# Another order of small matmuls inside their bursts, and Gelu ahead of a square on ScalarE, in a fused two-layer network

## The reference, cut to what matters

```python
x = attn_layer(shift_tokens(x), Wqkv[i], q_scale[i], k_scale[i], Wo[i]) + x
x = ffn_layer(shift_tokens(x), ln_g[i], ln_b[i], W1[i], b1[i], W2[i], b2[i]) + x
...
# attn_layer: 16 heads of 64, q and k normalised and rotated, windows of 32 tokens
sim = jnp.einsum('bhwie,bhwje->bhwij', bq, bk2) * QK_SCALE   # 32 queries x 64 keys
attn = jax.nn.softmax(sim, -1)
out = jnp.einsum('bhwij,bhwje->bhwie', attn, bv2)
...
# ffn_layer: 128 -> 2 x 341 -> 128
hg = xn @ W1 + b1
a, gate = jnp.split(hg, 2, -1)
return a * jax.nn.gelu(gate, approximate=False) @ W2 + b2
```

## Time and profile before

| | us |
|---|---|
| median of three runs | 1846.3 |
| lowest and highest | 1843.38 and 1856.85 |
| the profiled execution | 1840.72 |
| its span, first to last instruction | 1838.8 |

### The profile page before, as it was taken

How to read it: one execution, slowest core, us unless ns; L and a number is a source line. 1 busy time by engine, 2 the same in 40 slices (tenths; PEclk the granted TensorE clock), 3 DMA queues, 4 the chain that set the end, 5 groups by cost and what they waited for, 6 DMA issues and landing times. The chain is left out here.

```text
span 1838.8 us, 70687 instructions
## 1 busy us (share of the span) xinstructions
PE 1759.5 (96%) x30348; PEld 1138.0 (62%) x30348; DVE 1454.6 (79%) x1677; ACT 1161.2 (63%) x2031; POOL 1190.7 (65%) x1285
## 2 busy tenths in 40 slices
PE   7988999999999999999999999999999999998788
PEld 6855665665566666566566556656656656655466
DVE  6588788788788878888878878888787888886485
ACT  4356667667666765766766766666576676575554
POOL 1059677687677787767777767767776776775000
PEclk8899999999999999999999999999999999999999
DMA  4013222323222332223323223223223222222031
GB/s 149 1 50 78 56 72 68 91 66 78 73 67 62 93 80 74 68 56 94 80 66 80 64 65 99 67 67 80 69 59 91 71 75 69 66 68 76 2 70 48
DMA packets 87669, 128.94 MB, mean 70 GB/s; under 512 B 26776, under 2 KB 32800, under 8 KB 87360
## 3 DMA queue, kind: packets, MB, share of 16 engines
q1 hardware_dynamic: 87360, 124.43, 26.1%
HBM read 25.70 MB, written 1.11 MB: 15 GB/s over the span
## 5 line engine op out<-in xcount | busy, mean ns | idle before, releaser
L487 POOL TENSOR_TENSOR lent<-t,lent 128x1024 f32<-128x1024 f32 x192 | 455.2, 2371 | 355.8 <-DVE lent L955 355.2
L478 POOL TENSOR_TENSOR lent<-lent,rn 128x512 f32<-128x512 f32 x384 | 400.6, 1074 | 13.8
L618 PEld LDWEIGHTS sc_ps<-shared,v_win 64*64 64x64 f32 x12288 | 197.6, 135 | 147.8 <-issue 146.9
L570 PE MATMUL ring<-ident,lent 128*128 128x128 f32 x1536 | 241.3, 280 | 17.6 <-ACT gel L826 12.5
L570 PEld LDWEIGHTS ring<-ident,lent 128*128 128x128 f32 x1536 | 176.3, 140 | 131.4 <-issue 91.0
L495 POOL TENSOR_TENSOR shared<-shared,rden 128x512 f32<-128x512 f32 x192 | 196.5, 1045 | 90.1 <-DVE rden L939 90.1
L791 ACT ACTIVATE sq<-qk_ps 128x1024 f32<-128x1024 f32 x192 | 196.3, 1023 | 92.4 <-PE qk_ps L555 92.0
L784 ACT COPY shared<-ring 128x512 f32<-128x512 f32 x192 | 111.2, 580 | 197.4 <-PE ring L602 196.8
L955 DVE TENSOR_TENSOR lent<-qk_ps,rot 128x1024 f32<-128x1024 f32 x192 | 232.5, 1211 | 0.0
L965 DVE TENSOR_REDUCE sums<-sq 128x16 f32<-128x1024 f32 x192 | 231.8, 1208 | 0.0
L951 DVE TENSOR_TENSOR t<-qk_ps,rot 128x1024 f32<-128x1024 f32 x192 | 229.2, 1194 | 0.3 <-ACT sq L791 0.2
(11 more groups left out here) (209 smaller groups left out, 2665.2 us busy)
## 6 DMA issues: line engine op xcount, KB each, us to landing
v_win<-v_tok SPq DMA_DIRECT2D x1488, 64.0 KB
wqkv<-in_w_qkv SPq DMA_DIRECT2D x18, 512.0 KB, 3.7
spread<-gate_rows SPq DMA_DIRECT2D x32, 128.0 KB, 3.6
wo<-in_w_o SPq DMA_DIRECT2D x6, 512.0 KB, 4.0
w<-in_w SPq DMA_DIRECT2D x6, 341.0 KB, 3.2
w<-in_w SPq DMA_DIRECT2D x6, 192.0 KB, 2.9
r_xtok<-in_x SPq DMA_DIRECT2D x4, 256.0 KB, 4.2
out_x<-xo SPq DMA_DIRECT2D x4, 256.0 KB, 2.3
```

Source lines behind the costliest of these rows:

```text
L478: nc.gpsimd.tensor_tensor(by_head(quarter(qkn, f)), by_head(quarter(qkn, f)), rn[:, 8 * f:8 * (f + 1)].unsqueeze(2).to_broadcast([P, 8, DH ...
L487: nc.gpsimd.tensor_tensor(half(qkn, k), half(t1, k), half(t2, k), ALU.add).then_inc((q_added, k_added)[k], 1)
L570: ins = nc.tensor.transpose(to[:, n * P:(n + 1) * P], qkn[:, c * P:(c + 1) * P], ident[:, :])
L618: ins = nc.tensor.matmul(sc_ps[64 * par:64 * (par + 1), part, P * pair + WIN * q:P * pair + WIN * (q + 1)], v_win[64 * part:64 * (part + 1 ...
```

## The change

Three hunks. In `scores`, the loop over the four windows now goes inside a loop over `par_first`, and `par` alternates with the window. In `attend`, the four matmuls of a window come in another order. On ScalarE, Gelu 0 comes before the squares of q in stages with `up`. No instruction is added or removed, and no operand changes.

```diff
--- before.py
+++ after.py
@@ -583,8 +583,9 @@
                     if g > 1:
                         pe.wait_ge(oT_copied, 2 * (g - 1))
                 for pair in range(4 * f, 4 * (f + 1)):
-                    for q in range(TW):
-                        for par in range(2):
+                    for par_first in range(2):
+                        for q in range(TW):
+                            par = (par_first + q) % 2
                             ins = nc.tensor.matmul(
                                 sc_ps[WIN * q:WIN * (q + 1), par, 64 * pair:64 * (pair + 1)],
                                 qT[64 * par:64 * (par + 1), pair, WIN * q:WIN * (q + 1)],
@@ -612,14 +613,13 @@
                     pe.wait_ge(sc_sub, 2 * min(g + 2, TILE_COUNT))
                 for pair in range(2 * f, 2 * (f + 1)):
                     for q in range(TW):
-                        for par in range(2):
+                        for par, part in ((0, 0), (1, 1), (0, 1), (1, 0)):
                             n = 2 * pair + par
-                            for part in range(2):
-                                ins = nc.tensor.matmul(
-                                    sc_ps[64 * par:64 * (par + 1), part, P * pair + WIN * q:P * pair + WIN * (q + 1)],
-                                    v_win[64 * part:64 * (part + 1), TW * t + q, DH * n:DH * (n + 1)],
-                                    prT[64 * part:64 * (part + 1), n, WIN * q:WIN * (q + 1)],
-                                    start=True, stop=True)
+                            ins = nc.tensor.matmul(
+                                sc_ps[64 * par:64 * (par + 1), part, P * pair + WIN * q:P * pair + WIN * (q + 1)],
+                                v_win[64 * part:64 * (part + 1), TW * t + q, DH * n:DH * (n + 1)],
+                                prT[64 * part:64 * (part + 1), n, WIN * q:WIN * (q + 1)],
+                                start=True, stop=True)
                 if f == 1:
                     ins.then_inc(av_full, 1)
 
@@ -849,10 +849,9 @@
                     exponentials(g - 2, 1)
                 if up is not None:
                     nc.scalar.preload_act_table_set(GELU_SET)
+                    gelu(up, 0)
                 if tile_there(g):
                     squares(g, 0)
-                if up is not None:
-                    gelu(up, 0)
                 if tile_there(g - 1):
                     copy_qkT(g - 1, 1)
                 if tile_there(g):
```

## The result

The changed kernel takes 1833.0 us (median of 10 runs, 1826.3 to 1840.0) against 1850.6 us (10 runs, 1843.4 to 1857.7): a ratio of 0.9904, with a 95% interval of 0.9882 to 0.9926. The ratio stands for 17.8 us less (13.7 to 21.8), where 15.8 was forecast; the gain is clear of noise, and just inside the 1% that was called no change. The kernel before has a higher median over ten runs than over the three that the forecast stood on, 1850.6 against 1846.3.

What follows compares the result with a forecast made beforehand. TensorE, with work for 96% of the span, was taken to bound the kernel. Bursts 0, Gelu 0.64 plus 0.08 us, 0.72 x 22 = 15.8 us, off the three-run median 1846.3: 1830.5 us; range 1806 to 1850.

Steps and rivals of the forecast that it cites:

- The bursts cost nothing either way: AV (L618) and score (L588) bursts: the new orders of the first two hunks were each costed at 0.
- all four quadrants load weights at once: AV bursts: four records in 58 ns, each quadrant loading for its full time, so order can't fill them more; 0.
- The rival of neighbouring columns: Both bursts: neighbours sharing columns limit the pace; small case 17 us gained (1814), full 37 us (1793); chance 0.28.
- The rival of same-row neighbours: AV and score bursts: each same-row neighbour costs a step, 167 and 75 us in full, 2072 us; chance 0.12.
- Eight tiles full: First part of a score burst: eight records take about 56 ns, so all eight tiles are busy; scores costed at 0.
- Gelu ahead takes the wait of the transposes away: Feed-forward stages: Gelu 0 starts 0.92 us earlier, AV alone bounds the transposes, TensorE gains 0.64 us, 22 times.
- Gate 1 stays 1.66 us behind the transposes, so that surplus is lost: Next gate matmul needs the transposes' bank, copied by ScalarE, so the projection's gain beyond 0.64 us is lost.
- the upper end: Gelu stages: 20.2 us gained if all 0.92 us of Gelu's advance came through.
- The 0.08 us for the linear matmul's weight load: Before AV's second half: the weight load no longer waits for the copy of v; 0.08 us a stage.
- The squares of q are not missed: ScalarE: q's squares are ready 0.6 to 0.7 us later, but VectorE turns q only 4.5 us behind; lower end 0.
- The Gelu gain is given back: Rival, same stage: the transposes' copy comes late or GpSimd's scaling keeps its time; 1840 to 1848 us, chance 0.10.

Runs made afterwards that it cites:

- experiment 2: The kernel before with the first two hunks alone (new burst orders, Gelu unmoved): 1847.1 us against 1844.8, ratio 1.0012.
- experiment 3: The changed kernel with burst neighbours on the same rows wherever possible, in AV and scores: 1826.1 us, ratio 0.9908 to the kernel before.
- experiment 5: The changed kernel with every AV matmul cut in two along its moving side, 16 moving columns each, same 64 weight columns: 2077 us in one run.
- experiment 6: The changed kernel with every AV matmul cut in two along its weight side, 32 weight columns each, eight tiles in turn: 1998 us in one run.
- experiment 4: The changed kernel with AV's loops turned round, each quadrant getting the four windows of a pair in a row: 2084 us in one run.
- experiment 8: The changed kernel with every score matmul cut in two along its moving side, 32 moving columns each: 2144 us.
- experiment 7: The changed kernel with VectorE's product of Gelu 0 moved behind the sum of k's squares: 1830.7 us in one run.

## Why the prediction was right, and where it was not

- **The bursts cost nothing either way: right, and shown.** Experiments 2 and 3 leave the pace unchanged to the record. The reason given was that all four quadrants load weights at once, each for its full time. Experiments 5 and 6 show that AV's pace is the weight load, and experiment 4 fits a quadrant that takes its records in turn. The rival of neighbouring columns falls: experiment 2's interval leaves it 0.04% of the kernel, 1 us. The rival of same-row neighbours, the one that ended slower, has 0.3% left, 5 us of the 242 in its price.
- **"Eight tiles full" in the first part of a score burst: right, though the working clashes.** The prediction read 112 ns as the time of 128 weight columns for AV and, a paragraph on, as that of 128 moving columns for the scores. Both hold, since the earlier trace rows have as many or more weight columns than moving ones and experiment 8 shows the moving columns at work where they are the more. It also counts 192 AV bursts in one place and 190 in another; the trace has 192, and no result hangs on it.
- **Gelu ahead takes the wait of the transposes away: right.** 0.64 us forecast, 0.64 us in the trace, and AV alone bounds the transposes after the change.
- **"Gate 1 stays 1.66 us behind the transposes, so that surplus is lost": wrong.** Gate 1 comes 887.96 - 886.58 = 1.38 us behind them. I took the distance for a chain over ScalarE's copy of the transposes. But in the earlier trace rows that copy had begun at 887.88 and took 0.59, so it was there at 888.47, while gate 1 started at 888.88: it was not waiting for the copy but stood behind v's projection, which had itself waited for VectorE's product, and that for Gelu. Gate 1's first weight load did wait for the copy, but began 0.36 us ahead of its matmul (first row, before). After the change the copy ends at 887.86, the load follows at 887.91 (second row) and gate 1 starts at 887.96: now the copy bounds it, if narrowly, as v's projection would have let it start some 0.03 us sooner by the 0.86 us from gate 0 to linear 0.

```profile
888.52 0.19 PEld L649 LDWEIGHTS ring<-xn,w 128*128 128x128 f32 x1 [0.31 <-ACT qT L773]
```

```profile
887.91 0.30 PEld L649 LDWEIGHTS ring<-xn,w 128*128 128x128 f32 x2 [0.61 <-ACT qT L773]
```

  The whole 0.92 us of Gelu's advance came through, the upper end that the prediction had priced at 20.2 us. Experiment 7 shows the chain from the other side: a later product leaves the transposes alone and moves all that follows by 0.36 us.
- **The 0.08 us for the linear matmul's weight load** was counted beside the 0.64. Part of it is there (888.87 to 889.86 is 0.99 us, 1.03 before), but the total is set by the chain, so it was no term of its own.
- **The squares of q are not missed: right.** They end 0.6 us later (887.08 instead of 886.49), and the copy behind them still waits 0.20 us for its transposes. The stage's gain of 0.92 us shows that nothing on TensorE's way is held up by them.
- **The Gelu gain is given back: no.** The medians of the three other kinds of stages are unchanged to 10 ns.

By these terms the sum should have read 1850.6 - 20.2 = 1830.4 on the median of ten runs; the measurement gives 1833.0, and the kernel with the third hunk alone a ratio that stands for 21.4 us (16.8 to 26.0). That the forecast of 1830.5 is the same number is luck: its base, the median of three runs, was 4.3 us too low, and its gain 4.4 us too small. No version among these beats both kernels beyond its interval: the third hunk alone is as good as the whole change.

## What to carry to other kernels

Small matmuls on tiles of the array run side by side when the tiles take turns; count the tiles that are busy at once from the pace of the starts and the time that one record holds its tile before reordering neighbours, for if all are busy, no order helps, and four matmuls in a row on one tile hurt (2.25 us a burst instead of 0.92). Where one engine's result frees several things on TensorE's way, follow each of them to the last that starts late: here the wait that the profile named was 0.64 us of gain, the advance of the releaser 0.92, and all of the 0.92 came through. To ask what bounds an instruction, compare its start with the end of each of its releasers, not with the start of its neighbour.

## What the runs showed of the hardware that I had not expected

- **The look-ahead seems to pass over whole matmuls, but not far.** With the quadrants in turn, records start in groups of four, 7 ns apart, then 39 ns pass: 58 ns for four. Had each matmul's two records to start one behind the other on the same quadrant before the next matmul's, every second record would come 58 ns late. This takes the two records to stand side by side in the program, which the trace doesn't show. With four matmuls in a row on one quadrant, the burst takes 2.25 us instead of 0.92, not the 3.7 of no overlap at all.
- **Behind the first 32 records of a burst on eight tiles stands a hole,** 0.08 us with the scores as they are and 0.11 with 32 moving columns, and then the records come at 8 to 10 ns each whatever they cost the array (experiments 6 and 8). I read this as the rate at which TensorE gets its instructions; it hangs on their number and not on their columns, but what makes the hole stays open.
- **TensorE can run out of instructions.** Besides the hole there are waits for nothing that the profile names, at much the same places in every execution. A long one in a burst of 128 records of the changed kernel (TensorE, 14 records still to come):

```profile
941.73 1.45 PE L589 MATMUL sc_ps<-kT,qT 64*32 64x64 f32 x114
945.51 0.42 PE L589 MATMUL sc_ps<-kT,qT 64*32 64x64 f32 x14 [2.33 <-issue]
```

A transfer of the instruction queue (16 KB) begins at 942.76 and takes 1.46 us in this execution. It ends at 944.22, and 1.29 us later TensorE goes on. The other traces say the same. In all eleven there are 306 pauses of over 0.6 us between two records of one burst, and 304 of them end 1.15 to 1.65 us after such a transfer ended (the last one to end 0.5 us or more ahead); of moments taken at random, 7 to 10% do. The queue brings TensorE's instructions: it makes 242 transfers in the kernels with 60696 loads and matmuls for TensorE (two to a record), and 338 in the three that differ by 24576 more of them, one transfer for every 256. The DMA rows of the changed kernel's page and of experiment 8's (transfers, MB, share of the 16 engines):

```profile
q8 instruction: 242, 3.96, 1.0%
```

```profile
q8 instruction: 338, 5.54, 1.1%
```

So these are waits for the fetch of instructions. A score burst of 32 matmuls uses up 128 of them in 0.64 us, half a transfer, and a transfer mostly takes 0.9 to 1.5 us. What makes one fetch late and the next one not stays open. Together the waits explain most of the 9.0 us by which the two profiled executions differ beside the gain: inside the score bursts 18.8 us against 12.5.

- **A long wait for instructions can also cost clock.** In the execution before, the wait at the same place is 2.15 us long and the granted clock stays full. In the changed kernel's, a stretch at half the clock (1.2 instead of 2.4 GHz) follows for 3.4 us from 945.6, and again behind two other waits from 184.5 and 1211.9; two more waits of over 2 us, at 218 and 678, have none behind them. The execution before has none between 132 and 1685 us. TensorE behind the wait, before and then after:

```profile
945.38 1.12 PE L642 MATMUL ring<-xsq,mean_w 128*128 128x512 f32 x2
946.34 0.60 PE L602 MATMUL ring<-ident,shared 128*128 128x128 f32 x4
```

```profile
945.86 2.07 PE L642 MATMUL ring<-xsq,mean_w 128*128 128x512 f32 x2
947.73 1.06 PE L603 MATMUL ring<-ident,shared 128*128 128x128 f32 x4
```

From the first score record behind the wait to the next stage's first projection it takes 3.08 us (945.51 to 948.59) instead of 1.67 (945.11 to 946.78): the half clock costs 1.4 us there.
